# Layer 1's strip copies on another engine, and its block transposes over four PSUM banks

## The chip, the cores and the metric

One core of a Trainium2 chip runs the whole program. The metric is the device time of one execution in microseconds (us).

## The reference

The input is x, 16 samples of 128 channels by 32 x 32 pixels. Four layers follow one another, each as x = x + layer(groupnorm(x)), with 32 groups of 4 channels:

- Layer 0: one bilinear resampling at offsets that a 3 x 3 convolution yields, then a depthwise 3 x 3 and a pointwise convolution.
- Layer 1: a deformable convolution. The normalised image is averaged over 3 x 3 pixels; 3 x 3 convolutions of that average yield two offsets and a sigmoid mask for each of 9 taps and each pixel; each tap samples the average bilinearly at its offset place, times the mask; a 3 x 3 weight tensor (128 x 128 per tap) contracts the 9 samples and the channels.
- Layer 2: a dense 3 x 3 convolution with modified weights.
- Layer 3: attention from separable 7-tap filters with tanh kernels, gates and a pointwise output.

Everything is float32.

## The kernel before, in words

Channels lie on the 128 partitions. The kernel walks over 8 passes of two samples each (s = 0, 1); the first seven are the iterations of a hardware loop, the eighth is written out behind it. The order on every engine's queue is written by hand, with a semaphore for each hand-over. A pass does layer 1 of its two samples, layer 2, layer 0 of the next pass's samples, and layer 3.

Layer 1 does its bilinear sampling as matmuls. The averaged image of a sample (`img[s]`, 36 x 36 with its border) is cut into eight strips of 8 columns that start every 4 columns; they lie in one buffer, `strip8` (line 192), 128 partitions x 2304 elements, which both samples share. `strips` on GpSimd (line 425) fills it with one copy for each sample: it waits for the sample's average and, for sample 1, until all of sample 0's blocks have been transposed. The image is treated as 8 tiles of 16 rows by 8 columns. For each tile, `blocks` on TensorE (line 554) transposes four blocks of 128 pixels from `strip8` into one PSUM bank (4 matmuls of 128 columns, L567), and `blocks` on ScalarE (line 939) copies that bank, 512 elements, to its place in `xQ` (which shares the tile xq). The banks are the two halves of `psT` (line 216), taken in turn, so block n waits for the copy of block n-2. TensorE does all 8 tiles of sample 0 in one go (line 718), and those of sample 1 in pairs between the matmuls of sample 0's w1 convolution (lines 751 to 759). The line of a ScalarE copy is that of a helper, L900; its tiles tell copies apart: Gd for the offset parts, xq for the blocks, samp for the samples, strip from img for layer 0's strips (`strip12`, windows of 12 columns).

The order around it in a pass is this. TensorE: the offset convolution of sample 0 (L464, 36 matmuls into `psO0`), its products (L474, line 468), a doubling product (L575), the offset convolution of sample 1 (L464, into `psN`), the count of far offsets (L603), sample 0's blocks (L567), the offset products of sample 1 (L474), a branch on a flag (far offsets take another way, near ones go on), the near sampling of sample 0 (`near`, line 579, L596: 16 steps through two pairs of banks of `psN`, of which `psT` is one), and the w1 convolution of sample 0 into `psO0` (L490), and then sample 1. VectorE: the 3 x 3 averages (`pool3`, line 1284; its parts are L1297, L1299, L1301 and L1303), the store sum of each finished sample (L1627) at the pass's end; then the offset sum (L1423) that opens the next, the hats for the bilinear weights (L1397 to L1409), the flag (L1219), and for each tile a product (L1482) and a transpose (L1493), up to four tiles ahead of the sampling. ScalarE: offset parts of sample 0 (line 925), the mask (L998), offset parts of sample 1, sample 0's blocks, a copy after each sampling step, sample 1's blocks with its mask after the first two, normalisations (L922). GpSimd: besides the strips only the reciprocal roots of the norms (L422). SyncE issues all DMAs: a pass's input and output, 512 KB a sample.

`psO0` (line 213) is two banks. Sample 0's offset parts are in it until ScalarE has copied them, and the w1 convolution writes it after the sampling; between these it is not used.

Of the kernel before, what the change touches and what calls it, by code (L numbers as in the profile page):

```python
# [33 lines left out]
PW = W + 2 * PAD  # L34
TILES = 8
STRIPS = 4
# [7 lines left out]
QR = 4  # L44
QB = 2 * QR
QUADS = 16 // QR
PAIRS = 2
SIDES = SW // QR
# [67 lines left out]
def conv_preact_kernel(nc, x_d, ident_d, tab_d, vec_d, offb_d, w0off_d, w0dw_pw_d, w1off_d, w1_d, w2_d, r2_d,  # L116
                       win_d, win2T_d, cb1T_d, cb2T_d, kh_d, kv_d, woT_d, out_d):
    PASSES = x_d.shape[0] // 2
    with ExitStack() as ctx:
# [38 lines left out]
        img = [sb(f"img{s}", [C, PW, PW]) for s in range(2)]  # L158
# [57 lines left out]
        psT = psN[:, 2:4, :]  # L216
# [82 lines left out]
        def pair(u):  # L299

            return psN[:, 2 * (u % 2):2 * (u % 2) + 2, 0:K9 * QR * SW]

        def doubled(s, e):

            at = 4 + 27 * TILES * (1 - e)
            return ps[s][:, at:at + 27 * TILES]
# [55 lines left out]
        def wait_apart(eng, *waits):  # L362


            for signal, value in waits:
                eng.wait_ge(signal.sem, value)
            eng.sem_inc(passed[eng], 1)
# [41 lines left out]
        @block.gpsimd  # L409
        def _(pool):  # L410
            for each in signals:
                pool.sem_inc(each.sem, each.start)
            for t in (xn[0], xn[1], img[0], img[1], x2p, ahp, u3):
                nc.gpsimd.memset(t[:], 0.0).then_inc(borders_zero, 1)
            nc.gpsimd.memset(neg_half[:], -0.5).then_inc(borders_zero, 1)
            pool.wait_ge(borders_zero, 8)

            def rsqrt(i, name, order):
                g = norm(name)

                pool.wait_ge(var_ready.sem, var_ready.at(i, nth(name, order)))
                nc.gpsimd.tensor_tensor(out=g[:, 18:19], in0=g[:, 17:18], in1=neg_half[:],  # L422
                                        op=ALU.pow).then_inc(rstd_ready.sem, 1)

            def strips(i, s):

                wait_apart(pool, (pooled_ready, pooled_ready.at(i, s + 1)), (q_blkp, q_blkp.at(i, TILES * s)))
                whole = img[s][:]
                windows = bass.AP(whole.tensor, whole.offset, [whole.ap[0], [QR, STRIPS * SIDES], [PW, PW], [1, QB]])
                nc.gpsimd.tensor_copy(strip8[:], windows).then_inc(strip8_ready.sem, 1)  # L430

            def one_pass(i, more):
                for s in range(2):
                    strips(i, s)
                for name in EVENTS if more else LAST:
                    rsqrt(i, name, EVENTS if more else LAST)

            for name in FIRST:
                rsqrt(0, name, FIRST)
            if PASSES > 1:  # L440
                with pool.Fori(0, PASSES - 1) as i:
                    one_pass(i, True)
            one_pass(PASSES - 1, False)
# [3 lines left out]
        def _(pe):  # L447
# [106 lines left out]
            def blocks(i, s, places):  # L554

                pe.wait_ge(strip8_ready.sem, strip8_ready.at(i, s + 1))
                for n in places:
                    t, o = ORDER[n], TILES * s + n
                    if o >= 2:

                        pe.wait_ge(q_blk.sem, q_blk.at(i, o - 1))
                    dst = psT[:, n % 2, :]
                    for a in range(SIDES):
                        for e in range(PAIRS):
                            r0, m = 16 * (t % 2) + QR * e, PAIRS * a + e
                            block = strip8[:, SIDES * (t // 2) + a, r0:r0 + 16, :].rearrange("p r c -> p (r c)")
                            last = nc.tensor.transpose(dst[:, C * m:C * m + C], block, ident[:])  # L567
                    last.then_inc(q_blkp.sem, 1)
# [329 lines left out]
        def _(act):  # L898
            def copy(out, in_):
                return nc.scalar.activation(out, in_, ACT.Copy)  # L900
# [24 lines left out]
            def parts(i, n):  # L925

                s = n % 2
                act.wait_ge(parts_product.sem, parts_product.at(i, n + 1))
                for b in range(2):
                    last = copy(off_parts[s].rearrange("p (j b r c) -> p j b r c", b=2, j=STRIPS, c=SW)[:, :, b],  # L930
                                (psO[s] if n >= 2 else psT)[:, b, :].rearrange("p (r j c) -> p j r c", j=STRIPS, c=SW))
                last.then_inc(parts_ready.sem, 1)

            def wide(j, s, i, order):

                act.wait_ge(xn_ready.sem, xn_ready.at(i, nth(("S0", "S1")[s], order)))
                copy(strip12[s][:], wide_windows(img[s][:])).then_inc(wide_ready.sem, 1)

            def blocks(i, s, places):

                for n in places:
                    t, o = ORDER[n], TILES * s + n
                    act.wait_ge(q_blkp.sem, q_blkp.at(i, o + 1))
                    copy(xQ[:, t].rearrange("p a b c -> p (a b c)"), psT[:, n % 2, :]).then_inc(q_blk.sem, 1)

            def start_masks(j):
                for s in range(2):
# [42 lines left out]
            def one_pass(i, more):  # L990
                order = EVENTS if more else LAST
                parts(i, 2)
                for s in range(2):
                    if s:
                        blocks(i, s, range(2))
                    act.wait_ge(om2_ready.sem, om2_ready.at(i, s + 1))
                    for e in range(PAIRS):
# [805 lines left out]
```

## Time and profile before

| | us |
|---|---|
| median of 3 runs | 1814.29 |
| lowest, highest | 1813.67, 1815.27 |
| the profiled execution | 1814.15 |
| its span in the profile | 1812.3 |
| TensorE busy | 1668.3 (92%) |
| VectorE busy | 1189.5 (66%) |
| ScalarE busy | 601.8 (33%) |
| GpSimd busy | 83.9 (5%) |

The profile records one execution. Its span runs from the first to the last recorded instruction. Shares of busy time are means over stages with different limits; the timeline tells what each engine waited for. PE is TensorE's matmuls, DVE VectorE, ACT ScalarE, POOL GpSimd. "[0.43 <-ACT xq L900]" at a row's end says that the engine was idle for 0.43 us before it, and that this ended with ScalarE's instruction of line 900 that writes xq. Back-to-back instructions of an engine overlap a little, so start-to-start is the measure of pace. The granted clock is a share of TensorE's full 2.4 GHz.

### The profile page before, as it was taken

How to read it: one execution, taken by the hardware profiler on the slowest of the kernel's cores; microseconds unless marked ns; L12 is line 12 of the kernel's file. 1: busy time of each engine (PE TensorE's matmuls, PEld its weight loads, DVE VectorE, ACT ScalarE, POOL GpSimd, SP SyncE). 2: the span in 40 equal slices, each digit the busy share in tenths (PEclk: the TensorE clock that was granted, in tenths of full speed). 3: DMA queues.
4: the chain of work that ended last, by engine and by line, in shares of the span. 5: the costliest groups of instructions: out<-in, count | busy, mean ns of one | idle time of the engine just before them, and what ended most of it. 6: DMA issues, size and time to landing. Idle time of an engine off the chain costs nothing.

```text
span 1812.3 us, 23905 instructions
## 1 busy us (share of the span) xinstructions
PE 1668.3 (92%) x7908; PEld 861.0 (48%) x7908; DVE 1189.5 (66%) x2243; ACT 601.8 (33%) x986; POOL 83.9 (5%) x92
## 2 busy tenths in 40 slices
PE   4969999899999999999998999989999999989976
PEld 2535543555436553365534655345543555435422
DVE  5276359844698358883498735985459835797356
ACT  2125223341334413253242512434133441324222
POOL 1010000100000000000001000010000000000000
PEclk8989999999999999999999999999999999999988
DMA  3000000100001000000001000010000100000000
GB/s 108 12 12 2 1 0 1 49 1 1 1 14 37 1 1 1 34 15 2 1 1 49 2 1 1 1 49 1 1 1 2 48 2 1 1 24 1 1 0 24
DMA packets 7120, 22.97 MB, mean 13 GB/s; under 512 B 1232, under 2 KB 1936, under 8 KB 6928
## 3 DMA queue, kind: packets, MB, share of 16 engines
q1 hardware_dynamic: 6928, 20.58, 3.1%
q8 instruction: 99, 1.62, 0.4%
q14 instruction: 93, 0.76, 0.1%
HBM read 12.19 MB, written 8.39 MB: 11 GB/s over the span
## 4 chain that ended last, share of the span: by engine, by line
issue 74%; PE 15%; DVE 5%; POOL 3%; ACT 2%; POOLq 0%; DVEq 0%; ACTq 0%
PE psN L464 3%; POOL gst L422 2%; PE psO L490 2%; PE psO L464 1%; PE psN L567 1%; PE psN L490 1%; PE psO L687 1%; PE psN L687 1%; POOL strip L430 1%; ACT xq L900 1%; PE ps L474 1%; PE ps L575 1%; PE psN L596 1%; PE psN L816 1%; DVE samp L1554 1%
## 5 line engine op out<-in xcount | busy, mean ns | idle before, releaser
L490 PE MATMUL psN<-xn,w 128*128 128x512 f32 x576 | 277.2, 604 | 0.9 <-DVE yout L1319 0.9
L490 PE MATMUL psO<-samp,w 128*128 128x512 f32 x576 | 273.5, 605 | 0.0
L596 PE MATMUL psN<-GQt,xq 64*128 64x144 f32 x2048 | 165.4, 301 | 25.8 <-ACT samp L900 25.1
L900 ACT ACTIVATE samp<-psN 128x576 f32<-128x576 f32 x256 | 152.7, 648 | 86.8 <-PE psN L596 86.8
L596 PEld LDWEIGHTS psN<-GQt,xq 64*128 64x128 f32 x2048 | 138.3, 186 | 55.8 <-ACT samp L900 42.1
L1227 DVE COPY xblk<-psN 120x256 f32<-120x256 f32 x128 | 54.3, 424 | 155.5 <-PE psN L532 155.5
L1063 ACT ACTIVATE samp<-psN,vec 128x512 f32<-128x512 f32 x160 | 110.0, 687 | 129.7 <-PE psN L816 129.7
L490 PEld LDWEIGHTS psO<-samp,w 128*128 128x128 f32 x576 | 100.5, 191 | 94.5 <-issue 89.2
L490 PEld LDWEIGHTS psN<-xn,w 128*128 128x128 f32 x576 | 98.9, 190 | 81.7 <-issue 81.7
L687 PE MATMUL psN<-img,w 128*128 128x512 f32 x288 | 133.5, 609 | 0.0
L687 PE MATMUL psO<-img,w 128*128 128x512 f32 x288 | 132.9, 603 | 0.0
L900 ACT ACTIVATE G<-psN 120x256 f32<-120x256 f32 x128 | 49.1, 383 | 228.6 <-PE psN L538 228.6
L1482 DVE TENSOR_TENSOR GTs<-hf 128x576 f32<-128x576 f32 x128 | 106.2, 840 | 15.5 <-DVE flag L1219 11.2
L922 ACT ACTIVATE xn<-x,gst 128x1024 f32<-128x1024 f32 x32 | 40.2, 1257 | 227.2 <-DVE gst L1172 227.2
L422 POOL TENSOR_TENSOR gst<-gst,neg_half 128x1 f32<-128x1 f32 x64 | 41.5, 648 | 1475.4 <-DVE gst L1161 1475.4
L1493 DVE STREAM_TRANSPOSE GQt<-GTs 128x576 f32<-128x576 f32 x128 | 98.0, 770 | 13.9 <-PE psN L596 13.9
L900 ACT ACTIVATE xq<-psN 128x512 f32<-128x512 f32 x128 | 69.6, 597 | 77.8 <-PE psN L567 77.8
L816 PE MATMUL psN<-samp,kh_w 128*128 128x512 f32 x160 | 79.7, 639 | 8.4 <-DVE samp L1554 8.4
L687 PEld LDWEIGHTS psO<-img,w 128*128 128x128 f32 x288 | 53.7, 189 | 68.3 <-issue 68.3
L687 PEld LDWEIGHTS psN<-img,w 128*128 128x128 f32 x288 | 51.9, 188 | 69.8 <-issue 69.8
L816 PE MATMUL psN<-samp,kv_w 128*128 128x512 f32 x160 | 77.5, 624 | 5.5 <-DVE samp L1554 5.5
L464 PE MATMUL psN<-img,w0off 128*32 128x512 f32 x576 | 75.8, 621 | 5.5 <-ACT img L922 4.2
(142 smaller groups left out, 2264.2 us busy)
## 6 DMA issues: line engine op xcount, KB each, us to landing
xin<-in_x SPq DMA_DIRECT2D x16, 512.0 KB, 3.5
out<-yout SPq DMA_DIRECT2D x16, 512.0 KB, 3.4
w<-in_w SPq DMA_DIRECT2D x2, 576.0 KB, 5.8
samp<-in_r SPq DMA_DIRECT2D x1, 576.0 KB, 7.3
tab<-in_tab SPq DMA_DIRECT2D x1, 494.0 KB, 5.0
kh_w<-in_kh SPq DMA_DIRECT2D x1, 320.0 KB, 6.0
kv_w<-in_kv SPq DMA_DIRECT2D x1, 320.0 KB, 6.2
woT<-in_woT SPq DMA_DIRECT2D x1, 256.0 KB, 7.0
```

The source lines that it names most:

```text
L422: nc.gpsimd.tensor_tensor(out=g[:, 18:19], in0=g[:, 17:18], in1=neg_half[:], op=ALU.pow).then_inc(rstd_ready.sem, 1)
L464: last = mm(dst[32 * g:32 * g + 32, h, :], w[:, k, :], window(src)(h, k), start=(k < 4), stop=(k >= K9 - 4), skip_group_check=True)
L490: last = mm(dst[:, h, :], wgt[:, k, :], rhs(h, k), start=(k == 0), stop=(k == K9 - 1))
L596: last = mm(pair(u)[:, g, :].rearrange("p (k r c) -> p k r c", k=K9, c=SW)[:, :, :, cols], xQ[rows, t, a, e, :], w[rows, e, :, :, cols], s ...
L687: ins = mm(dst[:, h, :], w0[:, k, :], window(img[s])(h, k), start=(k == 0), stop=(k == K9 - 1))
L816: mm(product(m), lhsT, rhs[:, HALF * h:HALF * h + HALF], start=True, stop=True)\
L900: return nc.scalar.activation(out, in_, ACT.Copy)
L922: nc.scalar.activation(inner(dst), src[:].rearrange("p (r c) -> p r c", c=W), ACT.Identity, bias=g[:, 20:21], scale=g[:, 19:20]).then_inc( ...
L1063: nc.scalar.activation(out, bank(m)[0:out.shape[0]], fn, **kw).then_inc(l3_act.sem, 1)
L1227: v_.tensor_copy(xblk[b][:].rearrange("p h c -> p (h c)"), psT[0:BLK, 1, 0:2 * C])\
L1482: v_.tensor_tensor(GQ[n % 2][:].rearrange("p (k a b) -> p k a b", a=QR, b=QB), hy[:, ORDER[n]].unsqueeze(3).broadcast_to((C, PAIRS * K9, Q ...
L1493: v_.transpose(GQt[o % RING][:].rearrange("p e k r c -> p (e k r c)"), GQ[(n - 1) % 2][:])\
```

## The change

The strip copies are taken from GpSimd's queue and put into ScalarE's, with the same windows and the same two waits: sample 0's right behind the copies of its offset parts, sample 1's behind sample 0's sampling and ahead of the first block copies of sample 1. GpSimd keeps the reciprocal roots. Sample 0's blocks go in turn to four banks, the two of `psT` and the two of `psO0` (blocks 0, 1, 4, 5 and blocks 2, 3, 6, 7), and block n waits for the copy of block n-4; sample 1's stay with the two banks of `psT`.

```diff
+        def block_bank(s, n):
+
+            return (psT[:, n % 2, :], psO0[:, n % 2, :])[n // 2 % 2 if s == 0 else 0]
...
-            def strips(i, s):
-
-                wait_apart(pool, (pooled_ready, pooled_ready.at(i, s + 1)), (q_blkp, q_blkp.at(i, TILES * s)))
-                whole = img[s][:]
-                windows = bass.AP(whole.tensor, whole.offset, [whole.ap[0], [QR, STRIPS * SIDES], [PW, PW], [1, QB]])
-                nc.gpsimd.tensor_copy(strip8[:], windows).then_inc(strip8_ready.sem, 1)
-
             def one_pass(i, more):
-                for s in range(2):
-                    strips(i, s)
                 for name in EVENTS if more else LAST:
                     rsqrt(i, name, EVENTS if more else LAST)
...
                     t, o = ORDER[n], TILES * s + n
-                    if o >= 2:
-
-                        pe.wait_ge(q_blk.sem, q_blk.at(i, o - 1))
-                    dst = psT[:, n % 2, :]
+                    turns = 2 if s else 4
+                    if n >= turns:
+
+                        pe.wait_ge(q_blk.sem, q_blk.at(i, o - turns + 1))
+                    dst = block_bank(s, n)
...
+            def strips(i, s):
+
+                act.wait_ge(pooled_ready.sem, pooled_ready.at(i, s + 1))
+                act.wait_ge(q_blkp.sem, q_blkp.at(i, TILES * s))
+                whole = img[s][:]
+                windows = bass.AP(whole.tensor, whole.offset, [whole.ap[0], [QR, STRIPS * SIDES], [PW, PW], [1, QB]])
+                copy(strip8[:], windows).then_inc(strip8_ready.sem, 1)
+
             def blocks(i, s, places):
...
-                    copy(xQ[:, t].rearrange("p a b c -> p (a b c)"), psT[:, n % 2, :]).then_inc(q_blk.sem, 1)
+                    copy(xQ[:, t].rearrange("p a b c -> p (a b c)"), block_bank(s, n)).then_inc(q_blk.sem, 1)
...
                 parts(i, 2)
+                strips(i, 0)
                 for s in range(2):
                     if s:
+                        strips(i, 1)
                         blocks(i, s, range(2))
```

## Rows read from the trace of the kernel before

**Rows 1.** The page's head: the span, and busy time by engine.
```profile
span 1812.3 us, 23905 instructions
PE 1668.3 (92%) x7908; PEld 861.0 (48%) x7908; DVE 1189.5 (66%) x2243; ACT 601.8 (33%) x986; POOL 83.9 (5%) x92
```

**Rows 2.** Timeline, TensorE, pass 3: start, us, instruction, shape, count, [idle before, releaser].
```profile
755.19 6.26 PE L464 MATMUL psO<-img,w1off 128*32 128x512 f32 x36 [2.63 <-DVE img L1303]
...
772.37 1.07 PE L567 MATMUL psN<-ident,strip 128*128 128x128 f32 x8
773.88 1.15 PE L567 MATMUL psN<-ident,strip 128*128 128x128 f32 x8 [0.43 <-ACT xq L900]
...
776.56 1.15 PE L567 MATMUL psN<-ident,strip 128*128 128x128 f32 x8 [0.20 <-ACT xq L900]
777.54 1.87 PE L474 MATMUL ps<-tab,Gd 128*128 128x27 f32 x16
779.34 1.25 PE L596 MATMUL psN<-GQt,xq 64*128 64x144 f32 x16
780.85 1.30 PE L596 MATMUL psN<-GQt,xq 64*128 64x144 f32 x16 [0.26 <-ACT samp L900]
...
795.87 1.04 PE L567 MATMUL psN<-ident,strip 128*128 128x128 f32 x8
796.74 1.02 PE L490 MATMUL psO<-samp,w 128*128 128x512 f32 x2
```

**Rows 3.** Timeline, ScalarE, pass 3.
```profile
767.15 0.42 ACT L998 ACTIVATE mk<-om 128x72 f32<-128x72 f32 x2 [4.58 <-DVE om L1417]
...
773.22 1.09 ACT L900 ACTIVATE xq<-psN 128x512 f32<-128x512 f32 x2
...
777.25 1.09 ACT L900 ACTIVATE xq<-psN 128x512 f32<-128x512 f32 x2 [0.26 <-PE psN L567]
...
790.73 1.19 ACT L900 ACTIVATE samp<-psN 128x576 f32<-128x576 f32 x2 [0.32 <-PE psN L596]
796.50 1.09 ACT L900 ACTIVATE xq<-psN 128x512 f32<-128x512 f32 x2 [4.58 <-PE psN L567]
```

**Rows 4.** Groups by line, ScalarE: busy us, mean ns of one, idle before.
```profile
L900 ACT ACTIVATE xq<-psN 128x512 f32<-128x512 f32 x128 | 69.6, 597 | 77.8 <-PE psN L567 77.8
...
L900 ACT ACTIVATE strip<-img 128x1728 f32<-128x1728 f32 x16 | 26.3, 1644 | 0.2
```

**Rows 5.** Timeline, GpSimd, pass 3.
```profile
755.39 2.10 POOL L430 COPY strip<-img 128x2304 f32<-128x2304 f32 x1 [1.82 <-DVE img L1303]
777.88 2.11 POOL L430 COPY strip<-img 128x2304 f32<-128x2304 f32 x1 [20.38 <-PE psN L567]
```

**Rows 6.** Timeline, VectorE, pass 3.
```profile
748.90 1.29 DVE L1297 TENSOR_TENSOR pool_v<-xn 128x1088 f32<-128x1088 f32 x1
...
756.25 2.39 DVE L1297 TENSOR_TENSOR pool_v<-xn 128x1088 f32<-128x1088 f32 x1
...
776.32 0.77 DVE L1493 STREAM_TRANSPOSE GQt<-GTs 128x576 f32<-128x576 f32 x1
777.12 0.76 DVE L1482 TENSOR_TENSOR GTs<-hf 128x576 f32<-128x576 f32 x1
...
778.60 1.99 DVE L1482 TENSOR_TENSOR GTs<-hf 128x576 f32<-128x576 f32 x1
```

**Rows 7.** Timeline, TensorE and then VectorE, pass 4.
```profile
971.15 4.63 PE L464 MATMUL psO<-img,w1off 128*32 128x512 f32 x36 [2.62 <-DVE img L1303]
976.96 1.97 PE L474 MATMUL ps<-tab,Gd 128*128 128x27 f32 x16 [1.18 <-ACT Gd L900]
...
980.33 0.38 DVE L1423 TENSOR_TENSOR om<-ps,offb 128x216 f32<-128x216 f32 x1 [0.69 <-issue]
```

**Rows 8.** Line L1423, all passes: idle before it by releaser, us, times.
```profile
  issue: 2.4, 3
```

**Rows 9.** Windows, pass 3: busy times by engine, granted clock, DMA share, GB/s.
```profile
756.00:758.00 2.00, 2.00 (x16) 0.68 (x12) 2.00 (x2) 0.00 (x0) 1.50 (x1) 0.50 0.35 135
```

## The prediction

> **What bounds the kernel now.** I read the page's head first: the span is 1812.3 us and TensorE is busy for 92% of it [rows 1]. So time is gained only where TensorE idles, or where it works at the lower clock. The profiled execution took 1814.15 us, 0.14 under the median of 1814.29 us; I count against 1814.3. The eight passes repeat, so I then read the timeline of one (pass 3, counted from 0) around the changed work, an engine at a time.
>
> On TensorE [rows 2] three things are to be seen. The first sample's block transposes (L567, 32 matmuls) run in four groups of two blocks, the first at 772.37, the second at 773.88 and the last at 776.56, with idle time of 0.43 and 0.20 us between them that ends with ScalarE's copy of such a block: two PSUM banks are filled, then TensorE waits until ScalarE has emptied one. The offset products (L474) follow at 777.54 and the near sampling (L596) at 779.34. From the first block to the sampling that is 6.97 us. The second sample's blocks are transposed inside the w1 convolution, two at a time: one such group starts at 795.87 and the next convolution matmul at 796.74, so eight of these matmuls take 0.87 us when nothing holds them.
>
> On ScalarE [rows 3] the block copies pair up, 1.09 us for two. A single one takes 597 ns [rows 4], so copies back to back start 0.49 us apart. ScalarE is idle before most of its groups. GpSimd [rows 5] runs the two strip copies, 2.10 us each, at 755.39 and 777.88.
>
> VectorE [rows 6] shows what the strip copies cost. The same vertical sum L1297 takes 1.29 us at 748.90 and 2.39 us at 756.25, where GpSimd's copy ends at 757.49 (755.39 + 2.10) and L1297 1.15 later; the sample product L1482 takes 0.76 us at 777.12 and 1.99 at 778.60, beside the second strip copy. Both read two SBUF operands. The Trainium skill (SBUF — State Buffer, Who interferes with whom) says that a VectorE instruction with two SBUF inputs and a GpSimd instruction that reads SBUF exclude each other for a whole instruction, the later one waiting; this case's trace agrees.
>
> **Part 1: strip copy of sample 0 moves to ScalarE.** It is queued behind the copies of sample 0's offset parts, which end at 762.57, 4.58 us ahead of the mask at 767.15 [rows 3]. Its price, from ScalarE's own copies [rows 4]: 597 ns for 512 elements from PSUM, 1644 ns for 1728 elements between SBUF tiles with the same kind of window. The slope is 0.861 ns an element, so 2304 elements take 2.14 us. The bounds are 1.9 us (the added 576 elements at half that slope) and 3.3 us (should the runs cost and not the elements: 1.644 x 2304/1728 x 12/8, with 8 columns to a run where there were 12). It ends near 764.7, in pass 3's times, ahead of that mask, and the first user of the strips is the transpose at 772.37. So it costs nothing: the 4.58 us of idle time cover it. Without that cover, the mask, and then VectorE's hats, would be late by the excess. No DMA moves.
>
> **Part 2: strip copy of sample 1 moves to ScalarE**, behind the last sampling copy, which ends at 791.92 (790.73 + 1.19), and in front of the first block copy at 796.50 [rows 3]. TensorE wants these strips at 795.87, ScalarE can deliver at 793.8 to 795.2, and part 4 moves both ends alike. Up to 3.9 us of copy are covered (795.87 - 791.92). What is queued behind it are block copies that wait for the very transposes it feeds. Nothing again.
>
> **Part 3: GpSimd gets off VectorE's port.** L1297 becomes 1.10 us shorter (2.39 against 1.29) and the third L1482 1.23 us. What is the first worth? After the pooling VectorE ends the pass with the store sum and starts the next with the offset sum L1423, for which TensorE waits. In pass 4 the products it needs ended at 978.93 (976.96 + 1.97), but L1423 started only at 980.33, behind VectorE's own queue [rows 7]. Of all passes, three show L1423 with an idle time that no other engine ended, 2.4 us in total [rows 8]: there VectorE sets the moment, and 1.10 us earlier work lets L1423 start at 979.23, still behind the products' end. So 3 x 1.10 = 3.3 us. In the passes where the first offset convolution runs partly at the low clock, TensorE is the later one and nothing comes of it.
>
> The second, the L1482 at 778.60, lies beside TensorE's wait-free start today, so alone it gives nothing; but part 4 needs it. Without it the third tile's operand would be ready at 781.3 (778.60 + 1.99 + 0.77 for the transpose), with it at 780.1.
>
> **Part 4: four banks for sample 0.** Blocks 0 to 3 need no wait, block n waits for copy n-4. TensorE at its own pace starts a block every 0.435 us (0.87 for two), so 8 take 3.5 us. ScalarE starts its first block copy at 773.22, frees block 0 at 773.82, then one every 0.49: blocks 4 to 7 could start at 773.86, 774.35, 774.84 and 775.33, and TensorE reaches them at 774.11, 774.55, 774.98 and 775.42. No wait is left. L474 then starts at 775.85 and takes 1.80 (779.34 - 777.54), so the sampling could start at 777.65: 1.67 us earlier. The last block copy ends at 773.22 + 7 x 0.49 + 0.60 = 777.25, which is before that; this margin is 0.4 us. The Trainium skill (ScalarE: Activation LUTs, What ACT_TABLE_LOAD costs) gives 186 ns + 0.833 ns an element and an overlap of 93 ns, which would put the last copy at 777.45, still in time; by its figures the sum stays the same and the margin halves.
>
> The sampling's tiles come every 1.51 us, VectorE's every 1.48. The first transposed operand is there at 777.09 (776.32 + 0.77) [rows 6], the third at 780.1 and wanted at 777.65 + 3.02 = 780.7. So VectorE keeps up, with 0.6 us to spare.
>
> What no row shows is how long TensorE's queue takes from the last wait through the L474 products and the far/near branch. Today the last wait ends near 776.5 with ScalarE's sixth copy and the sampling starts 2.8 us later, with the engine busy all the while; so the queue needs 0 to 2.8. After the change that wait ends at 775.33, so the sampling starts by 778.2 at the latest: the gain is 1.17 to 1.67 us a pass. I take 1.6, since the engine never idled before L596 and the low end needs the queue to be exactly the limit. 8 x 1.6 = 12.8 us. What follows (the w1 convolution, TensorE alone) moves forward with it.
>
> **Clock.** A stretch such as 756 to 758 is granted 0.50, that is 1.2 GHz, after TensorE idled ahead of the offset convolution [rows 9]. The first offset convolution takes 6.26 us in pass 3, and 4.63 in pass 4 [rows 2, 7]. Which pass gets which will change, as every pass starts earlier. I take no gain or loss, and for the bounds three passes better or worse by that difference of 1.63 us: 4.9 us either way.
>
> **Sum.** 12.8 + 3.3 = 16.1 us, 1814.3 - 16.1 = 1798.2 us. A change of 0.2% (3.6 us) is about what can be told from none.
>
> **Rivals.**
> A. The sampling starts only half as much earlier, since the branch or ScalarE's last copy sets it. Today it starts 1.00 after the last block copy ends (777.25 + 1.09 = 778.34) [rows 3]; were that fixed, it would start at 778.25, a gain of 1.09. For it: copy and sampling are close. Against: L474 fills that time fully. 8 x 1.09 + 3.3 = 12.0 us, 1802.3 us. Chance 0.12.
> B. VectorE's long instructions have another cause than GpSimd's copy and stay. Then the third operand at 781.3 meets a demand at 780.7, a loss of 0.6 of 1.6, and the 3.3 go: 8 us, 1806.3 us. Against it: both kinds stretch only beside L430. Chance 0.04.
> C. Nothing comes of the banks, the sampling is bound by something that I don't see, and only part 3 counts: 3.3 us less, 1811.0 us, within 0.2%. Chance 0.05.
> D. Slower: the strip copy on ScalarE, with its short runs, costs far more than its elements. From 3.9 us on TensorE waits in the convolution for strips of sample 1, and ScalarE's queue holds the block copies behind it. From 3.9 + 1.6 + 0.4 = 5.9 us on the whole gain is gone; at 6.7 us the time is 1814.3 + 8 x 0.8, about 1821 us. For it: no row has runs of 8 columns on ScalarE. Against: 12-column runs cost 0.95 ns an element, and GpSimd's take 2.10. Chance 0.02.
> E. The low clock falls on more passes, three more of them, the rest as forecast: 1803.1 us. Chance 0.07.
>
> The forecast has 0.70. Its own range with the clock's bounds and 1.17 to 1.67 is 1793 to 1805; A and E lie in it, so it holds the time a little over 8 times in 10. Faster by over 0.2%: 0.92, within: 0.06, slower: 0.02.
>
> **What would show it.** Right: no L430 in GpSimd's rows; a ScalarE strip copy of 2304 elements at 2.1 us; L1297 and L1482 nowhere above 1.4 and 0.8; L567 of sample 0 as one run of 32 with no idle time, 5.3 us from its start to L596 instead of 6.97; idle ahead of L1423 never without a releaser for over 1 us past L474's end. Wrong: a copy above 3.9 us, L596 waiting for GQt or xq, or the convolution waiting for strips; or the start of passes not 1.6 to 2.7 us closer.

## The result and the profile after

The changed kernel takes 1798.27 us (median of 4 runs, 1795.01 to 1798.49) against 1814.68 for the kernel before (4 runs, 1813.67 to 1815.27): a ratio of 0.9907, interval 0.9894 to 0.9919, 16.4 us less. The forecast was 1798.2. That the two agree so closely is partly luck: the total was met, several of its terms were not, as the following shows, and two later comparisons of the same two kernels gave 19.4 and 17.4 us. The profiled execution took 1798.49 us with a span of 1796.7, beside 1814.15 and 1812.3 before.

The page's head, answering to [rows 1]:

```profile
span 1796.7 us, 23863 instructions
PE 1662.0 (93%) x7908; PEld 864.5 (48%) x7908; DVE 1170.8 (65%) x2243; ACT 632.8 (35%) x1002; POOL 49.2 (3%) x76
```

GpSimd has lost 16 instructions and 34.7 us of work, ScalarE has gained 16 and 31.0 us, and VectorE, whose work is the same, is busy 18.7 us less: its instructions no longer stretch (the two lengthenings of [rows 6], 1.10 and 1.23 us, would make 18.6 in eight passes). TensorE is busy 6.3 us less at the same count of matmuls, which already says that more than idle time went: some matmuls ran at a higher clock.

Three views of the changed kernel show the small steps. First the groups by line, ScalarE (as [rows 4]), then two lines of VectorE over all passes (count, shortest, median and longest in ns), the vertical sum and the sample product of [rows 6].

```profile
L896 ACT ACTIVATE strip<-img 128x2304 f32<-128x2304 f32 x16 | 34.0, 2125 | 3.0 <-ACT samp L896 3.0
```
```profile
L1303 DVE TENSOR_TENSOR pool_v<-xn x16: 1277/1283/1293, 102.5 to 1605.6; 128x1088 f32<-128x1088 f32 x16
```
```profile
L1488 DVE TENSOR_TENSOR GTs<-hf x128: 749/758/760, 127.6 to 1661.8; 128x576 f32<-128x576 f32 x128
```

The strip copy costs 2.125 us where 2.14 was forecast, and no VectorE instruction of either kind is longer than 1.29 and 0.76 us; before, the longest took 2.40 and 2.67.

TensorE in pass 3, answering to [rows 2]:

```profile
748.97 6.26 PE L459 MATMUL psO<-img,w1off 128*32 128x512 f32 x36 [2.62 <-DVE img L1309]
756.41 1.97 PE L469 MATMUL ps<-tab,Gd 128*128 128x27 f32 x16 [1.18 <-ACT Gd L896]
758.86 1.00 PE L571 MATMUL ps<-om,tab 128*128 128x216 f32 x4 [0.47 <-DVE om L1429]
759.78 4.62 PE L459 MATMUL psN<-img,w1off 128*32 128x512 f32 x36
...
764.57 1.07 PE L563 MATMUL psN<-ident,strip 128*128 128x128 f32 x8
765.48 1.04 PE L563 MATMUL psO<-ident,strip 128*128 128x128 f32 x8
766.35 1.04 PE L563 MATMUL psN<-ident,strip 128*128 128x128 f32 x8
767.23 1.04 PE L563 MATMUL psO<-ident,strip 128*128 128x128 f32 x8
768.10 1.87 PE L469 MATMUL ps<-tab,Gd 128*128 128x27 f32 x16
770.68 3.98 PE L592 MATMUL psN<-GQt,xq 64*128 64x144 f32 x32 [0.72 <-DVE GQt L1499]
```

Three things are to be seen. The four groups of block transposes follow each other without a wait, psN and psO in turn, and the offset products are done 5.40 us after the first block (768.10 + 1.87 - 764.57). The sampling then waits 0.72 us for VectorE's first transposed tile, which it never did before. And the second sample's offset convolution, 5.87 us long in the same pass before, takes 4.62: full clock.

VectorE in the same pass shows whose wait that is:

```profile
759.89 0.67 DVE L1423 COPY om<-ps 128x216 f32<-128x216 f32 x2 [0.75 <-PE ps L571]
...
760.77 2.15 DVE L1403 TENSOR_TENSOR hf<-tab,om 128x288 f32<-128x288 f32 x4
762.96 1.96 DVE L1408 SCALAR_TENSOR_TENSOR hf<-hf 128x1728 f32<-128x1728 f32 x1
764.95 1.06 DVE L1410 TENSOR_SCALAR hf<-hf 128x1728 f32<-128x1728 f32 x1
766.04 1.36 DVE L1415 SCALAR_TENSOR_TENSOR hf<-hf,mk 128x1152 f32<-128x1152 f32 x1
767.53 0.16 DVE L1225 CAST flag<-ps 128x1 int32<-128x1 f32 x1
768.42 1.43 DVE L1488 TENSOR_TENSOR GTs<-hf 128x576 f32<-128x576 f32 x2 [0.73 <-DVE flag L1225]
769.77 0.77 DVE L1499 STREAM_TRANSPOSE GQt<-GTs 128x576 f32<-128x576 f32 x1
```

From the doubling product (758.86) to the first sample product (768.42) it is 9.56 us in one chain: the wait for the doubling product, then the hats almost without a gap, then 0.73 us of idle time behind the flag's cast. Nothing of the change touches it. Where the doubling product runs at full clock, the chain takes 9.5 to 9.6 us (9.3 in pass 7); where that product takes 1.7 to 1.8 us, as in passes 2, 4 and 5 before, 10.4.

To find all of the time, I cut every pass at three events: S is from the start of the first offset convolution to the first block transpose, N from there to the start of the near sampling, M from there to the w1 convolution. What follows in a pass is 180.0 us in both kernels. Added over the eight passes, from the traces, in us:

| | before | after | after - before |
|---|---|---|---|
| up to pass 0's first offset convolution | 105.81 | 107.73 | +1.92 |
| S | 138.58 | 128.85 | -9.73 |
| N | 55.74 (6.97 each) | 45.01 (5.3 or 6.1) | -10.73 |
| M | 95.01 | 96.17 | +1.16 |
| rest, and the end after pass 7's w1 start | 1417.16 | 1418.94 | +1.78 |

N is the banks' term. In passes 0, 2, 4, 5 and 7 it is 5.32 to 5.38 us, in passes 1, 3 and 6 it is 6.11 or 6.12.

S splits at the start of the doubling product. Up to there the sum falls from 77.56 to 75.08, by 2.5 us: this is the part where VectorE's own queue had been late. From there to the blocks it falls from 61.02 to 53.77, by 7.2 us, and this part is the doubling product and a convolution, TensorE alone. Its two forms in the trace of the changed kernel are rows such as these, passes 1 and 2, TensorE:

```profile
333.26 4.62 PE L459 MATMUL psN<-img,w1off 128*32 128x512 f32 x36
...
545.40 6.26 PE L459 MATMUL psN<-img,w1off 128*32 128x512 f32 x36
```

Before, no pass had the 4.62 form for this second convolution: it took 5.35 to 6.78 us in all of them, the longest in pass 2, and this in pass 3:

```profile
549.45 6.78 PE L464 MATMUL psN<-img,w1off 128*32 128x512 f32 x36
...
766.34 5.87 PE L464 MATMUL psN<-img,w1off 128*32 128x512 f32 x36
```

The kernel before was traced once, so its pattern is that of one execution.

### The profile page after: what moved, and what is told of

Its sections match the earlier page's. It is cut to its first block, busy times and chain, and to the rows that moved or that the text cites. A ratio compares the mean times of both kernels' runs of the same rounds, so it can differ in the third digit from the quotient of the medians.

```text
span 1796.7 us, 23863 instructions
## 1 busy us (share of the span) xinstructions
PE 1662.0 (93%) x7908; PEld 864.5 (48%) x7908; DVE 1170.8 (65%) x2243; ACT 632.8 (35%) x1002; POOL 49.2 (3%) x76
## 4 chain that ended last, share of the span: by engine, by line
issue 83%; PE 10%; DVE 3%; POOL 2%; ACT 1%; POOLq 0%; DVEq 0%; ACTq 0%
PE psO L485 2%; POOL gst L426 2%; PE psN L812 1%; PE psN L485 1%; PE psN L683 1%; PE psO L683 1%; PE psN L459 1%; DVE samp L1560 1%; PE psN L592 1%; PE psO L545 0%; ACT samp L896 0%; PE ps L469 0%; PE psN L862 0%; PE psN L527 0%; PE psO L459 0%
## 5 line engine op out<-in xcount | busy, mean ns | idle before, releaser
L1488 DVE TENSOR_TENSOR GTs<-hf 128x576 f32<-128x576 f32 x128 | 95.6, 757 | 15.5 <-DVE flag L1225 11.2
L545 PE MATMUL psO<-G,xblk 120*128 120x128 f32 x512 | 79.8, 279 | 1.1
```

Of the source, the lines that this page charges most:

```text
L545: last = mm(psO[0][:, p // 4, C * (p % 4):C * (p % 4) + C], xblk[p % 2][:, u, :], G1[p % 2][:, u, :], start=(u == 0), stop=(u == 1))
L1488: v_.tensor_tensor(GQ[n % 2][:].rearrange("p (k a b) -> p k a b", a=QR, b=QB), hy[:, ORDER[n]].unsqueeze(3).broadcast_to((C, PAIRS * K9, Q ...
```

## The experiments

My theory was the prediction's, with two additions once the traces lay side by side: the time in S is mostly clock that fell otherwise, and the sampling is now bound by VectorE's chain in the passes whose second convolution runs at full clock. The rivals were that either part of the change alone makes the whole gain, and that the strip copy on ScalarE costs something that the gain hides. All ratios are to the kernel before in the same comparison, with 95% intervals.

### The changed kernel again

No edit.

> The changed kernel once more, for a second trace. Theory K (the low-clock stretches fall on other passes in every execution, since the program's start is not tied to them; they are worth a few us of the gain): 1795 to 1799 us, but the passes in which the first or second offset convolution takes over 6 us are not the same ones as in the first trace of it; the times from the first offset convolution to sample 0's first block take values near 15.6, 15.8 and 17.2 us again. Rival (which passes are slow is fixed by the kernel's own order): the same passes are slow, the times within 0.1 us of the first trace.

Measured: 1795.05 us (1794.07 to 1796.33), 0.9892 [0.9875, 0.9908]. Sums: S 130.50, N 44.78, M 96.12, the start 105.17. The passes' pattern is nearly that of the first trace, but pass 6 is a slow one here, pass 7 opens with the slow convolution, and the time before pass 0 is 2.6 us shorter. Neither theory holds whole: in these traces most passes keep their form, and two do not. A third trace of this kernel, of the run beside the halves below, has the 4.62 form in passes 1, 4 and 6. In all three traces it comes in three passes of eight, and in each of these the sampling waits for VectorE, 0.5 to 0.7 us. So single executions of one kernel differ by such steps: over three comparisons its runs lie between 1794.1 and 1800.2 us. Differences under about 3 us between variants are not read from medians below.

### Only the strip copies on ScalarE

```diff
-            return (psT[:, n % 2, :], psO0[:, n % 2, :])[n // 2 % 2 if s == 0 else 0]
+            return psT[:, n % 2, :]
...
-                    turns = 2 if s else 4
+                    turns = 2
```

> Only the strip copies move to ScalarE; sample 0's blocks keep two banks. Theory S (the port gives 1.10 us where VectorE opens the pass late, three or four passes, and the rest of the shortening before the blocks is the clock's): from the first block to the sampling 6.97 us in all passes; the opening offset sum never more than 8.1 us behind the start of the first offset convolution where that took 4.6 us; 1806 to 1811 us in all. Rival (the shorter times before the blocks, 9.7 us over eight passes, come from the port alone): about 1805 us, and the second offset convolution at 4.6 us in nearly all passes. Rival N (no gain without the banks): 1814 us.

Measured: 1808.01 us (1806.48 to 1809.46), 0.9965 [0.9951, 0.9979], 6.4 us less than before. N is 6.96 or 6.97 in every pass, as before, and M 95.01, as before. S is 130.34 instead of 138.58. The offset sum opens at 8.1 us into the pass where the first convolution is fast, in pass 4 for instance 8.07 instead of 9.18, and such passes have S of 15.8 to 15.9 where before they had 16.9 to 18.3 (pass 7, shorter in both kernels, 15.57 for 16.02). Part 3 of the prediction works by itself, and is worth more than its 3.3 us. In this trace the sum up to the doubling product falls by 5.9 us and not by 2.5, since five passes open with the fast convolution. Before, a fast one brought the doubling product no sooner (9.6 to 9.9 us into passes 1 to 6 either way); without the stretched sum it does.

### Only the four banks

The kernel before with the two edits of the banks alone.

```diff
+        def block_bank(s, n):
+
+            return (psT[:, n % 2, :], psO0[:, n % 2, :])[n // 2 % 2 if s == 0 else 0]
...
-                    dst = psT[:, n % 2, :]
+                    dst = block_bank(s, n)
```

> Only the four banks; the strip copies stay on GpSimd. Theory S (the third sample product is still stretched by 1.1 to 1.9 us beside sample 1's strip copy, so that the sampling waits for VectorE's third tile for 0.5 us or more, and 1.64 us of block time is given back in part): blocks to sampling 5.3 us where VectorE is early, then idle time in the sampling that ends with GQt; 1804 to 1808 us. Rival (the two parts are independent and add): 1814.7 less 13 or so, about 1802 us, with no such idle time.

Measured: 1809.58 us (1807.31 to 1814.22), 0.997 [0.9958, 0.9981], 4.8 us less; I had expected 1804 to 1808. The trace is that of the slowest of the seven runs, 1814.22 us, 2.7 to 6.9 us over the six others; its mean granted clock is 0.965, theirs 0.966 to 0.970, so what the clock takes in it is more than usual. In it N falls to between 5.32 and 5.36, 13.1 us in all, and then M grows from 11.8 to between 12.7 and 14.0 in the first seven passes, 12.0 us in all. Pass 2 shows how, GpSimd first, then VectorE, then TensorE:

```profile
558.64 2.63 POOL L434 COPY strip<-img 128x2304 f32<-128x2304 f32 x1 [18.73 <-PE psO L572]
```
```profile
557.88 1.43 DVE L1487 TENSOR_TENSOR GTs<-hf 128x576 f32<-128x576 f32 x2 [0.73 <-DVE flag L1224]
559.22 0.77 DVE L1498 STREAM_TRANSPOSE GQt<-GTs 128x576 f32<-128x576 f32 x1
560.03 1.85 DVE L1487 TENSOR_TENSOR GTs<-hf 128x576 f32<-128x576 f32 x1
561.80 0.77 DVE L1498 STREAM_TRANSPOSE GQt<-GTs 128x576 f32<-128x576 f32 x1
```
```profile
560.14 1.25 PE L601 MATMUL psN<-GQt,xq 64*128 64x144 f32 x16
562.70 1.25 PE L601 MATMUL psN<-GQt,xq 64*128 64x144 f32 x16 [1.31 <-DVE GQt L1498]
564.21 2.10 PE L601 MATMUL psN<-GQt,xq 64*128 64x144 f32 x16 [0.26 <-ACT samp L905]
```
```profile
564.00:566.00 2.00, 1.79 (x16) 1.75 (x16) 1.93 (x4) 1.31 (x3) 0.00 (x0) 0.61 0.00 0
566.00:568.00 2.00, 2.00 (x20) 1.88 (x16) 1.97 (x4) 1.22 (x3) 0.00 (x0) 0.53 0.00 0
```

The blocks are done earlier, so GpSimd's strip copy for sample 1, which waits for them, starts earlier too. It now lies on VectorE's third product (560.03), which takes 1.09 us longer than its 0.76. Behind it in VectorE's queue stands the second tile's transpose (561.80), and for that TensorE waits 1.31 us. In the windows of this pass (columns as [rows 9]) the granted clock then falls to 0.61 and 0.53, and 16 matmuls that take 1.25 us at full clock take 2.10. Of the 2.2 us that M grows by in this pass, 1.05 are the wait, counted against the 0.26 us that stand between these groups anyway, and the rest is the clock. Passes 1, 4 and 5 have waits of 1.17 to 1.31 us like this one. Passes 0, 3 and 6 have a shorter one, put down to ScalarE's copy, which ended when the second tile did; pass 3:

```profile
779.48 3.97 PE L601 MATMUL psN<-GQt,xq 64*128 64x144 f32 x32 [0.82 <-ACT samp L905]
```

From start to start of the matmul groups the waits cost 6.2 us in the eight passes. The other 5.8 us of the 12.0 are the lower clock, in passes 0, 2, 3, 5 and 6. The two parts are not additive: alone they give 6.4 and 4.8 us, together 19.4 in this comparison and 16.4 in the first.

### One strip copy on GpSimd, the other on ScalarE

The changed kernel with one of the two calls moved back.

```diff
             def one_pass(i, more):
+                strips(i, 1)
...
                     if s:
-                        strips(i, 1)
                         blocks(i, s, range(2))
```

> Four banks, sample 0's strip copy on ScalarE, sample 1's back on GpSimd. Theory S (the damage in the run with the banks alone is done by sample 1's copy: it stretches the second tile's product, TensorE waits about 1.3 us for that tile, and a low-clock stretch follows in the sampling): from the sampling's start to the w1 convolution 12.7 to 14.0 us instead of 11.8, before the blocks as in the changed kernel (15.6 to 17.2 us a pass); about 1805 us, 8 to 12 more than the changed kernel. Rival (sample 0's copy did it, through a later start of VectorE's chain): 11.8 us there and 1797 us.

Measured: 1806.36 us (1805.7 to 1807.35), 0.9952 [0.9936, 0.9969]. N is 5.32 everywhere and M 102.96 instead of 96.17. TensorE, pass 3:

```profile
774.88 1.25 PE L600 MATMUL psN<-GQt,xq 64*128 64x144 f32 x16
777.35 1.25 PE L600 MATMUL psN<-GQt,xq 64*128 64x144 f32 x16 [1.22 <-DVE GQt L1506]
```

It is the same wait as with the banks alone, so that wait belongs to sample 1's copy. But here it stays at the wait: M is 12.76 in this pass, 0.95 more than 11.81, and the window behind the wait is granted full clock. The expectation had S as in the changed kernel; it is 136.4 us here, with the slow form of both convolutions in every pass. So of what this version loses against the changed kernel, 7.5 us lie there and 6.8 in M, and 2.4 come back in N.

```profile
778.00:780.00 2.00, 1.75 (x26) 1.47 (x24) 1.97 (x4) 1.53 (x3) 0.00 (x0) 1.00 0.00 0
```

The mirror image puts sample 0's copy back instead:

```diff
             def one_pass(i, more):
+                strips(i, 0)
...
                 parts(i, 2)
-                strips(i, 0)
```

> Four banks, sample 0's strip copy back on GpSimd, sample 1's on ScalarE. Theory S (sample 0's copy costs 1.10 us of VectorE's opening and a longer idle time of TensorE, with a low-clock stretch behind it; nothing in the sampling): 16.9 to 18.3 us before the blocks in the passes whose first offset convolution takes 4.6 us, where the changed kernel has 15.8; the sampling 11.8 us; about 1802 to 1804 us. Rival (the gain before the blocks was the clock's chance): as the changed kernel, 1795 to 1798 us.

Measured: 1800.50 us (1799.01 to 1803.8), 0.9927 [0.991, 0.9943]. M is 96.18, as with the whole change, and S is 133.77 instead of 128.85. In passes 2 and 5, whose first convolution is fast, the offset sum comes at 9.17 and 9.45 us and not at 8.1; pass 7 has 8.26 for 7.79. The time is below the 1802 to 1804 us that I had expected. So sample 0's copy costs the opening of the pass, and sample 1's the sampling.

### The strip copy doubled

Each sample's strip copy is made twice on ScalarE, the second behind the first, and TensorE waits for the second.

```diff
-        strip8_ready = signal("strip8_ready", 2)
+        strip8_ready = signal("strip8_ready", 4)
...
-                pe.wait_ge(strip8_ready.sem, strip8_ready.at(i, s + 1))
+                pe.wait_ge(strip8_ready.sem, strip8_ready.at(i, 2 * s + 2))
...
                 copy(strip8[:], windows).then_inc(strip8_ready.sem, 1)
+                act.wait_ge(strip8_ready.sem, strip8_ready.at(i, 2 * s + 1))
+                copy(strip8[:], windows).then_inc(strip8_ready.sem, 1)
```

> The changed kernel with each strip copy on ScalarE made twice, 2.12 us more each. Theory C (both copies lie in ScalarE's idle time: 2.23 us are left behind the first and 2.08 behind the second in pass 3): sample 0's costs nothing, or delays the mask by under 0.5 us; sample 1's makes the convolution wait for strips by 0 to 0.5 us a pass; 1798 to 1803 us in all. Rival (ScalarE's copies are on the path): 2.12 to 4.25 us a pass, 1815 to 1832 us.

Measured: 1808.08 us (1806.67 to 1808.58), 0.9962 [0.9948, 0.9976]. That is 10 to 13 us over the changed kernel and outside the 1798 to 1803 of the expectation; only 6.2 of it is where I looked for it. ScalarE and then TensorE, pass 3:

```profile
788.64 4.28 ACT L896 ACTIVATE strip<-img 128x2304 f32<-128x2304 f32 x2 [0.38 <-ACT samp L896]
```
```profile
793.06 1.06 PE L563 MATMUL psN<-ident,strip 128*128 128x128 f32 x8 [0.69 <-ACT strip L896]
```

The second copy for sample 1 ends 0.69 us too late for TensorE and the stretch from the w1 convolution to the second sampling grows by 0.88 us in passes 0 to 6. TensorE would have begun at 792.37 (793.06 - 0.69), 3.7 us after the copies' start: that is the cover, for the 3.9 us of the prediction. The rest is in S: all eight passes have 17.0 to 17.4, none the 15.6 of the changed kernel. TensorE and windows, pass 3, where the second convolution of the changed kernel took 4.62 us at a granted 1.00:

```profile
764.54 5.64 PE L459 MATMUL psN<-img,w1off 128*32 128x512 f32 x36
```
```profile
764.00:768.00 4.00, 4.00 (x26) 0.98 (x29) 3.18 (x8) 1.11 (x3) 0.00 (x0) 0.66 0.63 231
```

Is that the copy's doing? The next run tells in part: only sample 0's copy is made twice, and TensorE waits for the second.

```diff
...
+                if s == 0:
+                    act.wait_ge(strip8_ready.sem, strip8_ready.at(i, 1))
+                    copy(strip8[:], windows).then_inc(strip8_ready.sem, 1)
```

> The changed kernel with only sample 0's strip copy made twice. In the run with both made twice the second sample's copy explained 0.88 us a pass (7 us), and every pass had the slow form of both offset convolutions (17.1 us before the blocks). Theory P (which passes get the slow form depends on how long a pass is, and there every pass was 215.1 us long and met the low clock at the same place; sample 0's second copy is free): passes of both forms again, 1795 to 1800 us. Rival (the double copy of sample 0 delays the mask or the doubling product): 17.1 us in all passes, about 1801 us or more.

Measured: 1797.51 us (1797.0 to 1798.54), 0.9903 [0.9887, 0.992]: the time of the changed kernel. ScalarE, pass 3:

```profile
756.37 4.28 ACT L896 ACTIVATE strip<-img 128x2304 f32<-128x2304 f32 x2
760.72 0.42 ACT L1007 ACTIVATE mk<-om 128x72 f32<-128x72 f32 x2
```

The second copy fills just what was idle ahead of the mask, which stays where it was, 4.35 us after the copies' start, as in the changed kernel (756.25 and 760.60). S is 129.19, with the 15.6 form in three passes. The slow form of the run before was therefore not caused by the copy that comes ahead of those convolutions. What differs is that its passes are longer by 0.88 us and nearly all alike, 215.1 to 215.4 us, and meet the low clock at the same place each time. Whether the pass's length decides, or sample 1's second copy and the wait behind it, is not shown: neither was tested by itself, and the length is in part a result of the slow forms.

### Offset parts handed over in halves, twice

TensorE waits 1.18 us ahead of the offset products for ScalarE's two copies, since both wait for the whole convolution. Here each bank's copy starts when its half is done.

```diff
-        parts_product = signal("parts_product", 4)
+        parts_product = signal("parts_product", 8)
...
-                last.then_inc(parts_product.sem, 1)
+                    last.then_inc(parts_product.sem, 1)
...
-                act.wait_ge(parts_product.sem, parts_product.at(i, n + 1))
+                    act.wait_ge(parts_product.sem, parts_product.at(i, 2 * n + b + 1))
```

> The changed kernel, and TensorE hands each half of an offset convolution to ScalarE by itself, so that the copy of the first half runs beside the second half's matmuls. One copy, 0.55 us, less between the first offset convolution and its products (1.18 us of idle time there now). Theory H: the products start 0.55 us earlier; where VectorE opens the pass late only 0.25 of it is left; VectorE's chain to the sampling starts earlier by as much: 2 to 4.4 us less than the changed kernel, 1792 to 1795 us. Rival (VectorE's chain bounds the sampling and the clock takes the rest): no difference, 1795 to 1798 us.

Measured: 1793.58 us (1791.57 to 1796.45), 0.9883 [0.9866, 0.9899]. It had no run of the changed kernel beside it, so both were run again together.

> The changed kernel a third time, beside the next two on the same chip, for a fair comparison: 1794 to 1799 us.

> The kernel with the halves of the offset convolution handed over by themselves, once more beside the changed kernel. Theory H: 2 to 4.4 us less than the changed kernel in the same job. Rival (the difference between jobs was the clock's chance): within 1 us of it.

Measured: the changed kernel 1796.46 us (1794.1 to 1800.16), 0.9905 [0.9891, 0.9918]; the halves 1795.44 us (1793.08 to 1798.18), 0.9903 [0.9888, 0.9918]. The intervals overlap, and the difference of 1.0 us is the rival's: none that can be told. The trace shows the edit at work all the same, TensorE in pass 3 of the first of these runs:

```profile
747.66 4.64 PE L459 MATMUL psO<-img,w1off 128*32 128x512 f32 x36 [2.63 <-DVE img L1309]
753.00 1.97 PE L469 MATMUL ps<-tab,Gd 128*128 128x27 f32 x16 [0.70 <-ACT Gd L896]
756.16 1.76 PE L571 MATMUL ps<-om,tab 128*128 128x216 f32 x4 [1.20 <-DVE om L1429]
```

The wait is 0.70 instead of 1.18 us, and 0.4 of it comes back as a longer wait for the offset sum, 1.20 where the changed kernel has 0.78 in its pass 4, which opens alike, because VectorE is not ready sooner. In passes with a slow first convolution the doubling product does come 0.49 us sooner, but passes 3 and 5 of the second run have N of 6.1 still, and pass 7 5.9: they wait for VectorE's first tile.

### Part of VectorE's chain given to ScalarE

If VectorE's chain from the doubling product on bounds the sampling, shortening it must show in N. On top of the halves, ScalarE takes the absolute value of two thirds of sample 0's hats (1152 of 1728 columns), VectorE keeps 576.

```diff
+                        act.wait_ge(hx_raw.sem, hx_raw.at(i, 1))
+                        nc.scalar.activation(hf[s][:, TEK * QR:], hf[s][:, TEK * QR:], ACT.Abs).then_inc(hx_abs.sem, 1)
...
-                    own.step(v_.scalar_tensor_tensor(hf[s][:], hf[s][:], -1.0, hf[s][:], ALU.mult, ALU.max))
+                    if s == 0:
+                        dve.sem_inc(hx_raw.sem, 1)
+                        y = hf[s][:, 0:TEK * QR]
+                        own.step(v_.scalar_tensor_tensor(y, y, -1.0, y, ALU.mult, ALU.max))
+                        dve.wait_ge(hx_abs.sem, hx_abs.at(i, 1))
...
```

> As the run before, and sample 0's absolute value of the hats' column part (1152 of 1728 elements) is taken by ScalarE beside VectorE's row part (576). VectorE's chain from the doubling product to the first tile loses about 0.75 us (1.96 us become 1.2 with the hand-over). Theory V (where both offset convolutions leave TensorE early, it waits 0.7 to 0.85 us for VectorE's first tile, in about half of the passes): these waits nearly vanish, the sampling starts 5.3 to 5.5 us behind the first block in all passes, and the time falls by 2 to 5 us below the run before. Rival (VectorE's chain is not what the sampling waits for): no difference, or a loss where ScalarE's copies of sample 1's offset parts come later.

Measured: 1789.18 us (1786.54 to 1791.73), 0.9864 [0.9849, 0.9879]. Its interval lies below that of the halves and of the changed kernel in the same comparison; it is the fastest version found, 25 us under the kernel before. VectorE, pass 3, then TensorE:

```profile
757.26 0.76 DVE L1415 SCALAR_TENSOR_TENSOR hf<-hf 128x576 f32<-128x576 f32 x1 [0.16 <-DVE hf L1407]
758.48 1.06 DVE L1420 TENSOR_SCALAR hf<-hf 128x1728 f32<-128x1728 f32 x1 [0.46 <-ACT hf L1012]
...
761.94 1.43 DVE L1498 TENSOR_TENSOR GTs<-hf 128x576 f32<-128x576 f32 x2 [0.72 <-DVE flag L1229]
```
```profile
758.75 1.07 PE L565 MATMUL psN<-ident,strip 128*128 128x128 f32 x8
...
762.28 1.87 PE L471 MATMUL ps<-tab,Gd 128*128 128x27 f32 x16
764.21 1.25 PE L594 MATMUL psN<-GQt,xq 64*128 64x144 f32 x16
```

From the doubling product (753.03) to the first sample product it is 8.91 us instead of 9.56. N is 5.46 in this pass (764.21 - 758.75) and 5.32 to 5.47 in all, with a second convolution at full clock; no pass has 6.1. Beside the halves alone, N falls by 1.8 us (43.07 for 44.87) and M by 1.2 (94.93 for 96.15), of 4.2 us of span. The other 1.2 us and what the medians differ by beyond that (6.3 in all) I can't put to the edit; they are of the size of the steps that one kernel's executions differ by.

## Why the prediction was right, and where it wasn't

**Parts 1 and 2** held. The copy costs 2.125 us for a forecast of 2.14, no cost of its shorter runs can be seen, and both covers are there: a second copy for sample 0 is free and one for sample 1 costs 0.88 us a pass. Rival D is out by the price alone, 2.1 us against the 5.9 from which it decides.

**Part 4** held in its mechanism: eight blocks without a wait, N of 5.32 to 5.38 for the forecast 5.37 in five passes. The sampling starts as soon as the offset products are done, so TensorE's queue and branch need nothing beyond it and the upper bound, 1.67, was the right end (by its own rows it is 1.69, 779.34 - 777.65); rival A, and C with it, is refuted in five passes of eight. The step that failed is "So VectorE keeps up, with 0.6 us to spare". It was read from pass 3 of before, where the second convolution took 5.87 us. VectorE's chain starts with the doubling product and takes 9.56 us to the first sample product, however long the second convolution is; where that convolution takes 4.62, TensorE comes 1.2 us sooner and VectorE's first tile does not. In three passes it sets the start of the sampling, at a cost of 0.79 us each. So 10.7 us came from this part instead of 12.8. Two of the prediction's own signs of being wrong are there with it: L596 waits for GQt in these passes, and of the first seven passes three are not 1.6 to 2.7 us shorter (pass 3 by 1.26, passes 2 and 5 by 4.14 and 2.77). The version that shortens VectorE's chain shows that this wait is VectorE's: with it no pass has 6.1. The first operand's time, 777.09, was a number of that pass; it should have been counted from the doubling product, and the margin worked out for a pass at full clock as well.

The dependence on part 3 was seen and put too low. Without it the text had the third tile late by 0.6 us, with the copy on the product at 778.60; but the banks let the copy itself start sooner, it falls on the product ahead of that one, and the second tile is late. TensorE waits 0.8 to 1.3 us, 0.6 to 1.05 more than usual, and in five passes of the first seven the clock falls behind that wait and costs 1.1 to 1.2 more: 0.9 to 2.2 us a pass, 12.0 of the 13.1 us that the banks give in the one execution that was traced. In the median run 4.8 us are left. Rival B's premise, that these long instructions have another cause, is refuted by both halves of the split: with sample 1's copy on GpSimd only the sample products stretch (up to 2.23 us, L1297's like at most 1.29), with sample 0's only the vertical sum (up to 2.40, the products at most 0.76). Its size, 5 us lost of 12.8, would have been too small.

**Part 3** had the right mechanism and a term too small. In passes 2, 4 and 7 the doubling product comes 1.16, 1.07 and 0.45 us sooner, 2.7 in all for the forecast 3.3; in pass 7 the offset sum now starts with the end of the products it needs, 7.79 us into the pass, so no more was to be had. Pass 5, the fourth with a fast first convolution before, has a slow one now. But S fell by 9.7. The other 7.2 us lie between the doubling product and the blocks. Of these 2.5 are two passes of before (2 and 5) in which that stretch took 8.5 to 8.7 us instead of 7.3. This form appears in 2 of 4, 2 of 3 and 1 of 3 fast-first passes of the three kernels that have sample 0's copy on GpSimd (before, banks alone, and sample 0's back) and in none of the 8 of the changed kernel's first trace and of the strips alone. So it is likely part 3's too, by way of the clock, though that was only counted and not isolated. The remaining 4.8 us are the three passes with the second convolution at full clock.

**Clock.** "I take no gain or loss" was wrong in sign and size for this stretch: three passes of the eight gained 1.6 us each there, as much as the 4.9 us that the text kept as a bound, though in the second convolution and not in the first, which it had in mind. Against it stand +1.2 in the sampling of pass 3 and +3.7 before the first pass and behind the last one's w1 start, which the second trace of the changed kernel does not have (105.17 and 1417.03). The windows of pass 3 of the changed kernel show the former. The wait of 0.72 us ahead of the sampling is followed by a fall to 0.50, that is 1.2 GHz; in passes 1 and 6 the same wait is not, and M stays at 11.80.

```profile
770.00:772.00 2.00, 1.32 (x11) 1.35 (x13) 1.97 (x3) 0.00 (x0) 0.00 (x0) 0.69 0.00 0
772.00:774.00 2.00, 2.00 (x18) 1.87 (x18) 1.93 (x4) 1.30 (x2) 0.00 (x0) 0.50 0.00 0
```

Rival E, more passes at the low clock, went the other way. The range was added up too narrow: with 1.17 us a pass and the clock's bound against it the upper end is 1806.5 (1814.3 - 9.4 - 3.3 + 4.9) and not 1805, and rival B would have lain inside it.

**The sum**, then, in spans: banks -10.7, the opening -2.5, the second convolution's clock -7.2, the sampling's clock +1.2, start and end +3.7, together -15.6. The forecast had -12.8, -3.3 and 0. The errors of the clock (-2.4 over these three) and of VectorE's bound (+2.1) cancelled.

**The port.** The prediction cited the Trainium skill (SBUF — State Buffer, Who interferes with whom) for VectorE and GpSimd excluding each other. All runs here agree: with the copies on ScalarE the longest sample product takes 0.76 us, with them on GpSimd up to 2.67. It works both ways, since GpSimd's copy, alone 2.10 us, takes 2.50 and 2.63 us where it comes second.

What stays open is why the changed kernel gets full clock in the second convolution of three passes. Neither the strips alone nor the banks alone does, nor the run with both strip copies doubled or the one with sample 1's copy on GpSimd; the split with sample 0's copy on GpSimd and the one with that copy doubled do. Each of these was traced once. Where a pass begins relative to the low spells may decide; that is a guess, and nothing here sets it by itself.

## What to carry to other kernels

When a wait is removed from the engine that bounds the kernel, look for what is triggered earlier by it: here a copy on an idle engine moved onto another instruction of VectorE and took back over half of what had been won ahead of the sampling, and on ScalarE it did not. Work out the margin of the engine that is next in line for the fastest form that the passes can take, not for the pass that happens to be on the screen. And where the clock changes from pass to pass, take sums over all passes and a second trace of the same kernel before a term of a few microseconds is believed.

## What the runs showed of the hardware that was not expected

The granted clock falls in the same places of a loop in a pattern that depends on the pass, not only on the idle time ahead: the first convolution comes after the same 2.6 to 2.7 us of idle time in every pass after the first, and takes 4.6 us in some and 6.0 to 6.3 in others, in every kernel run here but two. In those two, both strip copies doubled and sample 1's on GpSimd, the passes after the first are nearly all of one length (215.1 to 215.2, and 215.0 to 215.2 us), and it is slow in all. Nor does a wait inside the sampling settle it: 1.31 us were followed by grants of 0.61 and 0.53 in pass 2 of the banks alone and 1.30 us by full clock in its pass 4, 1.22 us by full clock in pass 3 of the split, and 0.72 us by 0.50 in one of the three passes of the changed kernel that have it.

No extra cost of runs of 8 columns over runs of 12 shows in ScalarE's strided copies: 2125 ns for 2304 and 1644 ns for 1728 elements differ by 0.835 ns an element. The Trainium skill (ScalarE: Activation LUTs, What ACT_TABLE_LOAD costs) has 186 ns + 0.833 ns an element, by which an estimate for the larger copy is 2105 ns; the trace agrees within 1%.
